# Last stage of a Mamba, attention and mixture block: where k is rotated, how q is split, and which loads go ahead of the store

## The chip, the cores and the metric

The kernel runs on one core of a Trainium2 chip. The metric is the device time of one execution in microseconds (us), as the median of several runs. Lower is better.

## The reference

The input x has 32 sequences of 64 tokens with 512 features. Three residual layers follow each other, each behind a layer norm (the third is the mixture of 64 experts of rank 8, of which 16 are chosen per token):

```python
x = x + mamba(layernorm(x), in_proj_w, conv_w, ..., out_proj_w)
x = x + cross_attention(layernorm(x), ctx, ctx, pos, mask, Wq, Wk, Wv, Wo)
x = x + experts(layernorm(x), A_w, B_w, Wq_w, keys)

def cross_attention(query, key, value, position_ids, src_mask, Wq, Wk, Wv, Wo):
    q = (query @ Wq).reshape(nb, q_len, 32, 128)
    k = (key @ Wk).reshape(nb, q_len, 8, 128)
    v = (value @ Wv).reshape(nb, q_len, 8, 128)
    q = q * cos + rotate_half(q) * sin
    k = k * cos + rotate_half(k) * sin
    scores = q @ k.T / sqrt(128); scores[mask == 0] = -1e9
    return (softmax(scores) @ v) @ Wo
```

Everything is fp32. This case is about the cross attention of the last block of tokens.

## The kernel before

**Tiling.** The 2048 tokens are four blocks of 512. `one(i, mamba, attn, nxt)` is one stage on every engine: it does the Mamba layer of block i together with attention and mixture of block i-1. `iterations` (L420) calls it five times: i = 0 (Mamba alone), i = 1 and 2 (both, a hardware loop), i = 3 (both, with no next block), and i = 4, the **last stage**, with attention and mixture of block 3 alone (`mamba` is False there). The five engine programs are written out by hand and meet only in semaphores. Each engine works strictly in its own written order. A `Stage` counts events: `x.upto(block, n)` is the count after event n of a block.

**Attention.** The 32 query heads go in 16 pairs, two pairs for each of the 8 heads of k and v. `step(jj, p, tail)` (PE: L1587, ACT: L893, DVE: L1252, SP: L548) handles pair 2jj+p. In this text a half is one such step, **even half** for p = 0 and **odd half** for p = 1. In a step PE transposes the probabilities of this pair (`turn_probs`, L1531), adds the output product of the pair before (`project_o`), makes the scores of the next pair (L1526), multiplies the probabilities with v (`values`) and makes the q of the pair after that (`project_q`, L1479). ACT copies q out of PSUM with its halves swapped (`swap_q`), takes the exponentials and copies the result of `values` out (`evac_o`). DVE, in its order, masks the scores (L1187), takes their maximum (L1193), inverts the sums of the exponentials (L1197), scales the probabilities (`probs`, L1201), makes the low part of the output (`o_low`, L1242, tile oT_lo), rotates the q of two pairs ahead (`rope_q`) and, at the end of an even half, rotates the **next k** (`rope_k`, L1172: three 128x512 operations, L1142, L1143 and L1146, the third behind a wait for the other two). The k of jj+1 is read by the scores that PE makes in the odd half. In the last stage k and v come from DRAM, where the first stage had put them.

**Two parts.** In the last stage the products are made of split operands. A matrix is written as a high part (rounded to the fp32r type) and a low part (what is left), and three matmuls stand for one fp32 matmul (`PASSES`). The activations q are split as a whole (tiles qT_hi and qT_lo, which lie over xnT and sz). The weights are split by GpSimd, whose queue is POOL: `split` (L664) makes the high part with one operation (L666, TENSOR_SCALAR) and the low part with another (L668, TENSOR_TENSOR), per step one of wq (`split_wq`) and one of wo (`split_wo`). The first wq parts lie over the first half of hs, the second over the second half, which holds the normed tokens (xn2) that PE transposes into q at the end of a stage.

**From stage 3 to the last stage.** At the end of stage 3 PE makes the mixture's A product (L1772), transposes its gated result (`zgt`), makes the B product (L1784), transposes xn2 into the PSUM tile acc (L1430, `ln2t`) and the rotary rows (L1633). ACT copies acc to qT (L804) and, in the next stage, qT to qT_hi (L922). DVE subtracts in one operation of 2048 columns (L1216). ACT then copies the rotary rows (`rop`). The first `project_q` waits for all of that and for the first split of wq.

**Loads.** SP issues the loads in its written order. `load_wa` (L443) waits until GpSimd or PE has given the buffer back. The last thing of a stage is the store of the block's result, which waits for `outr`; the first thing of the next stage is the load of the first two wq and the first wo:

```python
                if attn:
                    for n in range(2):
                        load_wa(i, n, a["wq"][n])
                    load_wb(i, 0, a["wo"][0])
...
                if attn:
                    eng.wait_ge(outr.sem, outr.upto(blk, 0))
                    eng.dma_start(out[blk], xn).then_inc(s_out, 16)
```

Of the kernel before, what the change touches and what calls it, by code (L numbers as in the profile page):

```python
# [16 lines left out]
F32 = mybir.dt.float32  # L17
# [4 lines left out]
ALU = mybir.AluOpType  # L22
ACT = mybir.ActivationFunctionType
# [7 lines left out]
TT = T // P  # L31
NB = T // SEQ
KE = E // P
DIN, NS, KC, R = 1024, 16, 4, 32
DT_TILES = DIN // P
# [44 lines left out]
def build(nc, a, out):  # L80
    ctx = ExitStack()
    with ctx:
# [9 lines left out]
        def sem(name):  # L92
            return ctx.enter_context(nc.semaphore(name))
# [10 lines left out]
        qT = sb("qT", [P, KE, T])  # L104
# [73 lines left out]
        qT2 = over("qT_hi", [P, KE, T], "xnT", 0), over("qT_lo", [P, KE, T], "sz", 0)  # L178
# [7 lines left out]
        acc = pb("acc", [P, TT, 512])  # L186
# [2 lines left out]

        q2 = qr[:, :, :].rearrange("p h t -> p (h t)").rearrange("p (b q) -> p b q", q=2 * SEQ)  # L190

        def bank(n):

            return pq[:, n, :] if n < 2 else pk[:, n - 2, :]
# [134 lines left out]
        ordy = stage("o_ready", PAIRS)  # L329
        wod = stage("wo_done", PAIRS)  # L330

        s_acth = sem("activations_hi")
        s_actl = sem("activations_lo")
        wqh = stage("wq_hi", PAIRS)
        wqs = stage("wq_split", PAIRS)
# [17 lines left out]
        zgt = stage("z_transposed", KE)  # L353
# [8 lines left out]
        yr = stage("y_gated", DT_TILES)  # L362
        opd = stage("out_proj", TT)
# [5 lines left out]
        qTr = stage("qT_ready", KE)  # L369
# [69 lines left out]
        def _(eng):  # L439
# [3 lines left out]
            def load_wa(i, at, src):  # L443

                eng.wait_ge(wad, wa_base(i) + at + (LEAD - 1))
                eng.dma_start(wa[:, at % 2, :], src).then_inc(s_wa[at % 2], 16)
# [5 lines left out]
            def load_wb(i, at, src):  # L452
                eng.wait_ge(wbd, wb_base(i) + at + (LEAD - 1))
                eng.dma_start(wb[:, at % 2, :], src).then_inc(s_wb[at % 2], 16)
# [16 lines left out]
            def one(i, mamba, attn, nxt):  # L471
                at_z, at_x, at_a = wa_places(mamba, attn, nxt)
                at_o, at_b = wb_places(mamba, attn)
                blk = i - 1
                if attn:
                    for n in range(2):
                        load_wa(i, n, a["wq"][n])
                    load_wb(i, 0, a["wo"][0])
                if mamba:

                    eng.wait_ge(sstr.sem, sstr.upto(i, 0))
# [147 lines left out]
                if attn:  # L629
                    for n in range(W_KE):  # L630
                        load_wa(i, at_a + n, a["aw"][n])
                    for n in range(W_KE):
                        load_wb(i, at_b + n, a["bw"][n])
                if attn:
                    eng.wait_ge(outr.sem, outr.upto(blk, 0))
                    eng.dma_start(out[blk], xn).then_inc(s_out, 16)
# [6 lines left out]
        def _(eng):  # L643
# [18 lines left out]
            def one(i, mamba, attn, nxt):  # L662
# [7 lines left out]
                def split_wq(jj, o):  # L670
                    p = o % 2
                    eng.wait_ge(s_wa[p], (wa_half(i) + (o // 2 + 1) + jj) * 16)

                    eng.wait_ge(qd.sem, qd.upto(i - 1, o - 2) + jj * 2)
                    hold(eng)
                    split(wa[:, p, :], [x[:, :] for x in wq2[p]], wqh, wqs, lambda s: s.upto(0, o) + jj * 2)
                    eng.wait_ge(wqs.sem, wqs.upto(0, o) + jj * 2)
                    eng.sem_inc(wad, 1)
# [86 lines left out]
                if not mamba:  # L765

                    eng.wait_ge(yad.sem, yad.upto(i - 1, NS * NCH - 1))
                    split_wq(0, 0)
                    eng.wait_ge(ln2t.sem, ln2t.upto(i - 1, KE - 1))
                    split_wq(0, 1)  # L770
                    split_wo(0, 0)
                    steps(eng, split_step)
# [20 lines left out]
        def _(eng):  # L793
# [6 lines left out]
            def evacuate(to, banks, done, ready, b):  # L800

                for k in range(KE):
                    eng.wait_ge(done.sem, done.upto(b, k))
                    S.activation(to[:, k, :], banks(k), ACT.Copy).then_inc(ready.sem, 1)  # L804
# [15 lines left out]
            def one(i, mamba, attn, nxt):  # L820
# [94 lines left out]
                    if mamba and attn and not tail and p == 1:  # L915
                        evac_v(jj + 1)

                if not mamba:
                    eng.wait_ge(yr.sem, yr.upto(blk, DT_TILES - 1))

                    eng.wait_ge(qTr.sem, qTr.upto(blk, KE - 1))
                    S.activation(qT2[0][:, :, :], qT[:, :, :], ACT.Copy).then_inc(s_acth, 1)  # L922
                if attn:
                    prefill()
                if mamba:
# [103 lines left out]
                if attn:  # L1029
                    evacuate(zgT, bank, zgt, zgr, blk)  # L1030
                if mamba:
                    evacuate(qT, lambda k: acc[:, k, :], ln2t, qTr, i)

            iterations(eng, one)

# [2 lines left out]
        def _(eng):  # L1038
# [170 lines left out]
            def one(i, mamba, attn, nxt):  # L1209
                blk = i - 1  # L1210
                rope_q, rope_k, mask_scores, max_scores, invert_sum, probs = attention_of(blk, mamba)
                if not mamba:

                    eng.wait_ge(opd.sem, opd.upto(blk, TT - 1))
                    eng.wait_ge(s_acth, 1)
                    V.tensor_tensor(qT2[1][:, :, :], qT[:, :, :], qT2[0][:, :, :].bitcast(F32),  # L1216
                                    ALU.subtract).then_inc(s_actl, 1)
                if mamba and not attn:

                    eng.wait_ge(xnr.sem, xnr.upto(0, KE - 1))  # L1220
# [31 lines left out]
                def step(jj, p, tail):  # L1252

                    soft = attn and not (tail and p == 1)
                    if mamba:
                        if p == 0:
                            eng.wait_ge(ur.sem, ur.upto(i, NCH - 1))
                        eng.wait_ge(s_bc[p], i * (8 * NS) + jj * 16 + 16)
                        scan_input(i, jj, p, 0)
                        scan_input(i, jj, p, 1)  # L1260
                        scan(i, jj, p, 0)
                        scan(i, jj, p, 1)
                        times_c(i, jj, p, 0)
                    if soft:
                        mask_scores(jj, p + 1)
                    if mamba:
                        times_c(i, jj, p, 1)
                    if soft:
                        max_scores(jj, p + 1)
                    if mamba:  # L1270
                        scan_input(i, jj, p, 2)
                        scan_input(i, jj, p, 3)
                        scan(i, jj, p, 2)
                        scan(i, jj, p, 3)
                    if mamba:
                        times_c(i, jj, p, 2)
                    if soft:
                        invert_sum(jj, p + 1)
                    if mamba:
                        times_c(i, jj, p, 3)  # L1280
                    if soft and not mamba:
                        probs(jj, p + 1)
                    if not mamba:
                        o_low(jj, p)
                    if attn and not tail:
                        rope_q(jj, p + 2)
                        if p == 0:
                            rope_k(jj + 1)

                def scan_alone(jj, p, c):  # L1290
# [122 lines left out]
        def _(eng):  # L1413
# [3 lines left out]
            eng.wait_ge(s_ident, 2)  # L1417
            eng.wait_ge(s_init, 3)
            eng.wait_ge(s_const, 16 * 9)

            def accs(k):
                return acc[:, k, :]

            def turn(x, banks, normed, done, b):

# [36 lines left out]
            def one(i, mamba, attn, nxt):  # L1462
# [177 lines left out]
                if attn:  # L1640
                    if mamba:
                        eng.wait_ge(s_ctx, blk * 16 + 16)
                        project_v(0)
                    else:
                        eng.wait_ge(s_actl, 1)
                    eng.wait_ge(rop.sem, rop.upto(blk, 0))
                    eng.wait_ge(qTr.sem, qTr.upto(blk, KE - 1))
                    project_q(0, 0)
                    free_wa(0, 0)
# [219 lines left out]
```

## Time and profile before

| | |
|---|---|
| median of 3 runs | 2400.57 us (2399.07 to 2403.79) |
| span of the profiled execution | 2396.3 us, first to last instruction and landing (the page has no other time of that execution; the median is 4.2 us more) |
| mean granted TensorE clock | 0.942 of full |
| PE busy | 2107.1 us, 88% |
| DVE busy | 1786.4 us, 75% |
| ACT busy | 1059.8 us, 44% |
| POOL busy | 588.9 us, 25% |
| last stage | from about 2024 us to the end |

The busy shares are means over stages with different limits. The last stage is a sixth of the span: PE, DVE, ACT and POOL hand work to each other there in every half, and the waits between them, read in order of time, say more than the shares.

### The profile page before, as it was taken

The numbers are of one execution on the slowest core, as the hardware profiler recorded it, in microseconds if no ns is written. First come the engines' busy times: TensorE is split into PE (matmuls) and PEld (weight loads), VectorE is DVE, ScalarE is ACT, GpSimd is POOL, SyncE is SP. The second block draws the span as 40 slices with busy tenths as digits, with TensorE's granted clock in tenths as the row PEclk, the third lists the DMA queues.
The fourth block names the chain that finished last, engine by engine and source line by source line (L and its number), as shares of the span: only waits on it lengthen the run. The fifth ranks groups of instructions, "written<-read, shape, count | busy, mean of one in ns | idle before, by whom it ended". The sixth has DMA issues, their size and how long they took to land.

```text
span 2396.3 us, 27137 instructions
## 1 busy us (share of the span) xinstructions
PE 2107.1 (88%) x8244; PEld 1194.4 (50%) x8248; DVE 1786.4 (75%) x1801; ACT 1059.8 (44%) x2613; POOL 588.9 (25%) x405
## 2 busy tenths in 40 slices
PE   6877888989999979989999979989999987799987
PEld 2332453445555534445555534445555533577763
DVE  3499994389999975289999985279999984355533
ACT  2544441465565522365665522365655521243330
POOL 0099981001111120001111110001111120566530
PEclk9888999899999989899999989889999999799888
DMA  1468893148888771238888871238888772122210
GB/s 62 166 152 198 213 213 121 54 133 187 181 177 187 166 173 53 72 123 179 176 189 179 181 172 60 72 106 172 176 196 175 171 173 82 65 90 97 88 44 18
DMA packets 110074, 328.98 MB, mean 137 GB/s; under 512 B 12945, under 2 KB 13073, under 8 KB 107569
## 3 DMA queue, kind: packets, MB, share of 16 engines
q0 software_dynamic: 35328, 127.94, 28.7%
q1 hardware_dynamic: 68912, 189.58, 26.3%
q10 hardware_dynamic: 5760, 10.49, 1.2%
q8 instruction: 45, 0.74, 0.1%
q14 instruction: 29, 0.23, 0.0%
HBM read 183.00 MB, written 14.94 MB: 83 GB/s over the span
## 4 chain that ended last, share of the span: by engine, by line
DVE 40%; PE 31%; issue 18%; DMA 5%; ACT 3%; DVEq 1%; POOL 1%; SPq 1%; POOLq 0%; ACTq 0%; PEldq 0%
DVE hs L1130 13%; PE acc L1443 5%; DVE hs L1137 5%; DVE hs L1300 5%; PE pq L1488 4%; DMA xc<-hs 3%; DVE hs L1121 3%; DVE qr L1167 2%; PE pq L1732 2%; PE pq L1496 2%; PE pq L1526 2%; PE acc L1655 2%; PE pk L1732 2%; PE acc L1565 2%; DVE sc L1187 1%
## 5 line engine op out<-in xcount | busy, mean ns | idle before, releaser
L706 POOL DMA_DIRECT2D xc<-hs x192 | 165.8, 866 | 1301.6 <-DVE hs L1137 1263.9
L1130 DVE TENSOR_TENSOR_SCAN hs<-dA,hs 128x1024 f32<-128x1024 f32 x192 | 428.9, 2276 | 0.0
L888 ACT ACTIVATE dA<-dt,aneg 128x504 f32<-128x504 f32 x384 | 253.5, 707 | 250.9 <-DVE hs L1130 250.7
L1496 PE MATMUL pq<-qT,wa 128*128 128x512 f32 x768 | 354.8, 616 | 9.2 <-DVE sc L1187 9.2
L1576 PE MATMUL acc<-wb,oT 128*128 128x512 f32 x768 | 351.7, 602 | 3.6 <-ACT oT L876 3.6
L1137 DVE TENSOR_TENSOR hs<-hs,bc 128x1024 f32<-128x1024 f32 x256 | 307.9, 1205 | 2.2
L853 ACT ACTIVATE pr<-sc,mx 128x64 f32<-128x64 f32 x512 | 170.8, 335 | 247.4 <-DVE mx L1193 247.4
L1443 PE MATMUL acc<-xnT,wa 128*128 128x512 f32 x512 | 232.2, 607 | 11.5 <-PE acc L1443 4.4
L1496 PEld LDWEIGHTS pq<-qT,wa 128*128 128x128 f32 x768 | 146.9, 197 | 183.8 <-issue 173.7
L1121 DVE TENSOR_TENSOR hs<-u,bc 128x1024 f32<-128x1024 f32 x192 | 226.3, 1219 | 8.2 <-ACT xc L976 5.9
L1526 PE MATMUL pq<-kT,qp 128*128 128x64 f32 x1024 | 190.9, 289 | 41.2 <-DVE kT L1146 16.3
L1576 PEld LDWEIGHTS acc<-wb,oT 128*128 128x128 f32 x768 | 141.1, 193 | 147.5 <-issue 143.4
L1526 PEld LDWEIGHTS pq<-kT,qp 128*128 128x128 f32 x1024 | 159.0, 205 | 78.3 <-issue 61.2
L1443 PEld LDWEIGHTS acc<-xnT,wa 128*128 128x128 f32 x512 | 96.4, 193 | 145.5 <-issue 130.5
L1528 PE MATMUL pq<-k2T,qr 128*128 128x64 f32 x768 | 154.4, 284 | 0.0
L1528 PEld LDWEIGHTS pq<-k2T,qr 128*128 128x128 f32 x768 | 122.4, 201 | 0.0
L731 POOL TENSOR_TENSOR qp<-u,bc 128x1024 f32<-128x1024 f32 x32 | 92.9, 2904 | 107.8 <-ACT xc L976 107.6
L1187 DVE COPY_PREDICATED sc<-mask,pq 128x512 f32<-128x512 int32 x64 | 46.7, 729 | 88.3 <-PE pq L1528 45.6
L731 POOL TENSOR_TENSOR qr<-u,bc 128x1024 f32<-128x1024 f32 x32 | 100.2, 3130 | 7.6 <-DVE hs L1300 7.6
L1079 DVE SCALAR_TENSOR_TENSOR xc<-acc,cw,xc 128x504 f32<-128x504 f32 (+2 forms) x96 | 69.9, 734 | 42.1 <-ACT xc L811 39.6
L1510 PEld LDWEIGHTS pk<-wv,ctxT 128*128 128x128 f32 x768 | 87.5, 192 | 27.4 <-issue 26.4
L1510 PE MATMUL pk<-wv,ctxT 128*128 128x128 f32 x768 | 92.0, 278 | 7.7 <-ACT oT L876 7.7
(200 smaller groups left out, 3312.7 us busy)
## 6 DMA issues: line engine op xcount, KB each, us to landing
xc<-hs POOLq DMA_DIRECT2D x240, 512.0 KB, 6.9
bc<-bc_rows SPq DMA_DIRECT2D x64, 512.0 KB, 7.5
wa<-in_wq SPq DMA_DIRECT2D x64, 512.0 KB, 10.2
wb<-in_wo SPq DMA_DIRECT2D x64, 512.0 KB, 5.8
wa<-in_wx SPq DMA_DIRECT2D x16, 512.0 KB, 4.2
wa<-in_wz SPq DMA_DIRECT2D x16, 512.0 KB, 4.9
wb<-in_ow SPq DMA_DIRECT2D x16, 512.0 KB, 7.2
k<-k_rows SPq DMA_DIRECT2D x32, 256.0 KB, 11.1
```

Source lines behind the costliest of these rows:

```text
L731: G.tensor_tensor(inputs[c % 2].rearrange("p (d t) -> p d t", t=T), u[:, 2 * c:2 * c + 2, :], bc[:, p, 0:1, :].to_broadcast([P, 2, T]), AL ...
L853: ins = S.activation(pr[:, b, :], sc[:, b, :], ACT.Exp, bias=mx[:, b:b + 1], accum_out=sm[:, b:b + 1])
L888: ins = S.activation(to[:, :, 1:SEQ], dt[:, s, :].rearrange("p (b t) -> p b t", t=SEQ)[:, :, 1:SEQ], ACT.Exp, scale=aneg[:, s, bass.ds(jj ...
L1121: V.tensor_tensor(hs[:, c, :].rearrange("p (d t) -> p d t", t=T), u[:, 2 * c:2 * c + 2, :], bc[:, p, 0:1, :].to_broadcast([P, 2, T]), ALU. ...
L1130: V.tensor_tensor_scan(out=hs[:, c, :], data0=dA[:, c % 2, :], data1=hs[:, c, :], initial=0.0, op0=ALU.mult, op1=ALU.add).then_inc(scd.sem, 1)
L1137: V.tensor_tensor(h3, h3, bc[:, p, 1:2, :].to_broadcast([P, 2, T]), ALU.mult).then_inc(hcd.sem, 1)
L1443: ins = M.matmul(banks(s % 4), wa4((s // 2) % 2)[:, k, (s % 2) * P:(s % 2 + 1) * P], xnT[:, k, :], start=(k == 0), stop=(k == KE - 1))
L1496: ins = M.matmul(pq[:, h, :], wa4(p)[:, k, h * P:(h + 1) * P], qT[:, k, :], start=(k == 0), stop=(k == KE - 1))
L1510: ins = M.matmul(pk[:, 1, t * D:(t + 1) * D], ctxT[:, k, t * P:(t + 1) * P], wv[:, k, :], start=(k == 0), stop=(k == KE - 1))
L1526: ins = M.matmul(pq[:, 0, seq], qp[:, b, :], kT[:, seq], start=True, stop=not mamba)
L1528: ins = M.matmul(pq[:, 0, seq], q2[:, b, :], k2T[:, seq], start=False, stop=True)
L1576: ins = M.matmul(acc[:, t, :], oT[:, h, t * P:(t + 1) * P], wb2(o % 2)[:, h, :], start=False, stop=(stop and h == 1))
```

## The change

It has three parts.

1. **k.** In the last stage `rope_k(jj + 1)` stands in an even half between `max_scores` and `invert_sum` on DVE. It stood at the end of that half, behind `rope_q`. Stages with Mamba keep their order.
2. **q.** At the end of stage 3 ACT copies acc to qT_hi directly, four times 512 columns, behind a wait for the Mamba output (since qT_hi lies over a tile that it read). The copy to qT and the copy of 2048 columns are gone. DVE subtracts in four pieces of 512 columns, straight from acc in PSUM, each behind its own piece of ACT's.
3. **Loads.** The first two wq and the first wo of the next stage are issued at the end of a stage, ahead of the wait for the result and of its store. On GpSimd the first split of wq also waits for the first transposed piece of the mixture's gated result.

```diff
@@ SP, start of a stage
-                if attn:
-                    for n in range(2):
-                        load_wa(i, n, a["wq"][n])
-                    load_wb(i, 0, a["wo"][0])
@@ SP, end of a stage
+                if mamba:
+
+                    for n in range(2):
+                        load_wa(i + 1, n, a["wq"][n])
+                    load_wb(i + 1, 0, a["wo"][0])
                 if attn:
                     eng.wait_ge(outr.sem, outr.upto(blk, 0))
                     eng.dma_start(out[blk], xn).then_inc(s_out, 16)
@@ GpSimd
                     eng.wait_ge(yad.sem, yad.upto(i - 1, NS * NCH - 1))
+                    eng.wait_ge(zgt.sem, zgt.upto(i - 2, 0))
                     split_wq(0, 0)
@@ ACT
-                if not mamba:
-                    eng.wait_ge(yr.sem, yr.upto(blk, DT_TILES - 1))
-
-                    eng.wait_ge(qTr.sem, qTr.upto(blk, KE - 1))
-                    S.activation(qT2[0][:, :, :], qT[:, :, :], ACT.Copy).then_inc(s_acth, 1)
...
                 if mamba:
-                    evacuate(qT, lambda k: acc[:, k, :], ln2t, qTr, i)
+
+                    if not nxt:
+                        eng.wait_ge(yr.sem, yr.upto(i, DT_TILES - 1))
+                    evacuate(qT if nxt else qT2[0], accs, ln2t, qTr, i)
@@ DVE
-                    eng.wait_ge(opd.sem, opd.upto(blk, TT - 1))
-                    eng.wait_ge(s_acth, 1)
-                    V.tensor_tensor(qT2[1][:, :, :], qT[:, :, :], qT2[0][:, :, :].bitcast(F32),
-                                    ALU.subtract).then_inc(s_actl, 1)
+                    for k in range(KE):
+                        eng.wait_ge(qTr.sem, qTr.upto(blk, k))
+                        V.tensor_tensor(qT2[1][:, k, :], acc[:, k, :], qT2[0][:, k, :].bitcast(F32),
+                                        ALU.subtract).then_inc(s_actl, 1)
...
                     if soft:
                         max_scores(jj, p + 1)
+                    if not mamba and not tail and p == 0:
+                        rope_k(jj + 1)
...
                         rope_q(jj, p + 2)
-                        if p == 0:
+                        if mamba and p == 0:
                             rope_k(jj + 1)
@@ PE
-                        eng.wait_ge(s_actl, 1)
+                        eng.wait_ge(s_actl, KE)
```

What this does to the order of an engine, at three places. First DVE in an even half of the last stage, from the maximum to the end of the half. Before:

```order
L1193 TENSOR_REDUCE mx<-sc 128x8 [waits scores_read]
L1197 RECIPROCAL sm<-sm 128x8 [waits exp_done]
L1201 TENSOR_TENSOR pr<-pr,sm 128x512 [waits sum_inverted]
L1247 TENSOR_TENSOR oT_lo<-pk,oT_hi 128x512 [waits o_ready]
L1247 TENSOR_TENSOR oT_lo<-pk,oT_hi 128x512
L1162 REGISTER_ALU
L1142 TENSOR_TENSOR qp<-pq,cosT 128x2x8x64 [waits scores_done,q_swapped]
L1143 TENSOR_TENSOR qr<-qr,sinT 128x1024
L1146 TENSOR_TENSOR qp<-qp,qr 128x2x8x64 [waits q_times_sin,q_times_cos]
L1173 ISA
L1174 ISA [waits k_loaded]
L1176 ISA [waits k_halves_loaded]
```

In the changed kernel the same stretch reads (all lines of the code are two further down there):

```order
L1195 TENSOR_REDUCE mx<-sc 128x8 [waits scores_read]
L1176 ISA [waits k_loaded]
L1178 ISA [waits k_halves_loaded]
L1144 TENSOR_TENSOR kT<-k,cosT 128x512 [waits scores_done]
L1145 TENSOR_TENSOR kr<-kr,sinT 128x512
L1148 TENSOR_TENSOR kT<-kT,kr 128x512 [waits k_times_sin,k_times_cos]
L1199 RECIPROCAL sm<-sm 128x8 [waits exp_done]
L1203 TENSOR_TENSOR pr<-pr,sm 128x512 [waits sum_inverted]
L1249 TENSOR_TENSOR oT_lo<-pk,oT_hi 128x512 [waits o_ready]
```

The three operations of k now stand ahead of the inversion, the scaling and the low part of the output.

Second ACT at the end of stage 3, from the copy of q. Before:

```order
L804 ACTIVATE qT<-acc 128x512 [waits ln2_transposed] x4
L922 ACTIVATE qT_hi<-qT 128x2048 [waits qT_ready,y_gated]
L846 ACTIVATE sc<-zeros 128x512 [waits exp_done]
L933 ACTIVATE cosT<-pq 128x512 [waits rotary_transposed]
L934 ACTIVATE sinT<-pq 128x512
```

In the changed kernel:

```order
L808 ACTIVATE qT_hi<-acc 128x512 [waits ln2_transposed,y_gated]
L808 ACTIVATE qT_hi<-acc 128x512 [waits ln2_transposed] x3
L850 ACTIVATE sc<-zeros 128x512 [waits exp_done]
L932 ACTIVATE cosT<-pq 128x512 [waits rotary_transposed]
L933 ACTIVATE sinT<-pq 128x512
```

The copy of 2048 columns is gone from between the copies of q and those of the rotary rows.

Third SP from the mixture's weights of stage 3 on. Before:

```order
L454 DMA wb<-in_bw 128x1024 [waits wb_used] x2
L636 DMA out<-dt 128x4x512 [waits out_ready]
L446 DMA wa<-in_wq 128x1024 [waits wa_used] x2
L454 DMA wb<-in_wo 128x1024 [waits wb_used]
L502 DMA xa<-xr 128x2048 [waits out_ready,ln2_done]
```

In the changed kernel:

```order
L456 DMA wb<-in_bw 128x1024 [waits wb_used] x2
L448 DMA wa<-in_wq 128x1024 [waits wa_used] x2
L456 DMA wb<-in_wo 128x1024 [waits wb_used]
L639 DMA out<-dt 128x4x512 [waits out_ready]
L500 DMA xa<-xr 128x2048 [waits out_ready,ln2_done]
```

The store and its wait for the result now stand behind the three loads.

## Rows read from the trace of the kernel before

**Rows 1.** Chain of waits, 1850 us to the end: shares by line.

```profile
by line: PE pq L1488 18.6%; issue 13.0%; PE acc L1565 7.0%; DVE hs L1130 6.9%; PE pq L1526 6.4%; PE acc L1772 5.2%; PE pk L1552 3.7%; PE pq L1784 2.7%; PE pq L1732 2.7%; DMA xc<-hs 2.5%; PE pk L1784 2.5%; PE pk L1732 2.5%; DVE hs L1137 2.3%
```

**Rows 2.** Timeline of PE, into the last stage: start, us, line, tiles, count, [idle before].

```profile
2006.89 1.44 PE L1430 MATMUL pq<-ident,dt 128*128 128x128 f32 x8
...
2026.30 1.04 PE L1633 MATMUL pq<-ident,oT 128*128 128x128 f32 x8
2037.47 0.77 PE L1488 MATMUL pq<-qT_hi,wq_hi 128*128 128x512 f32 x1 [10.13 <-POOL wq_lo L668]
...
2052.04 3.68 PE L1526 MATMUL pq<-kT,qp 128*128 128x64 f32 x16 [6.50 <-DVE qp L1146]
```

**Rows 3.** Timeline of ACT, same place.

```profile
2025.19 2.07 ACT L804 ACTIVATE qT<-acc 128x512 f32<-128x512 f32 x4 [15.19 <-PE acc L1430]
2027.35 1.91 ACT L922 ACTIVATE qT_hi<-qT 128x2048 fp32r<-128x2048 f32 x1
...
2030.16 0.59 ACT L934 ACTIVATE sinT<-pq 128x512 f32<-128x512 f32 x1
```

**Rows 4.** Timeline of DVE, same place.

```profile
2029.37 2.29 DVE L1216 TENSOR_TENSOR qT_lo<-qT,qT_hi 128x2048 fp32r<-128x2048 f32 x1 [4.25 <-ACT qT_hi L922]
...
2032.18 1.53 DVE L1143 TENSOR_TENSOR kr<-kr,sinT 128x512 f32<-128x512 f32 x1
```

**Rows 5.** Timeline of SP's queue, same place.

```profile
2025.59 1.56 SPq L446 DMA_DIRECT2D wa<-in_wq  x2
```

**Rows 6.** Timeline of POOL, same place.

```profile
2031.90 3.00 POOL L666 TENSOR_SCALAR wq_hi<-wa 128x1024 fp32r<-128x1024 f32 x1 [41.89 <-DMA wa<-in_wq]
2034.99 2.34 POOL L668 TENSOR_TENSOR wq_lo<-wa,wq_hi 128x1024 fp32r<-128x1024 f32 x1
```

**Rows 7.** Windows of the last stage: stretch, length, busy of PE, PEld, DVE, ACT, POOL, clock, DMA, GB/s.

```profile
2073.41:2108.90 35.49, 33.41 (x173) 27.60 (x175) 16.96 (x21) 12.73 (x42) 10.50 (x4) 0.91 0.24 82
2108.90:2312.47 203.57, 187.87 (x1009) 154.32 (x1008) 104.52 (x126) 76.41 (x252) 122.21 (x46) 0.94 0.23 79
2193.52:2208.48 14.96, 14.84 (x86) 12.34 (x87) 7.20 (x9) 6.37 (x21) 8.79 (x4) 1.00 0.57 194
2260.95:2278.77 17.82, 17.80 (x85) 15.03 (x85) 8.03 (x9) 6.37 (x21) 8.56 (x4) 0.81 0.39 133
2278.77:2296.22 17.45, 14.87 (x85) 12.11 (x85) 9.73 (x12) 6.37 (x21) 12.55 (x5) 1.00 0.25 90
```

**Rows 8.** Who waited for whom, 2108.9 to 2312.4 us: total us, times, longest.

```profile
PE pq L1526 <- DVE kT L1146: 14.4, 6, 2.4
```

**Rows 9.** Timeline of DVE, one even half (scores begin at 2278.77 us).

```profile
2281.78 0.69 DVE L1193 TENSOR_REDUCE mx<-sc 128x8 f32<-128x512 f32 x1
2285.30 0.20 DVE L1197 RECIPROCAL sm<-sm 128x8 f32<-128x8 f32 x1 [2.83 <-ACT pr L853]
...
2286.26 1.29 DVE L1247 TENSOR_TENSOR oT_lo<-pk,oT_hi 128x512 fp32r<-128x512 f32 x2
...
2294.73 1.34 DVE L1146 TENSOR_TENSOR kT<-kT,kr 128x512 f32<-128x512 f32 x1
```

**Rows 10.** Timeline of POOL, the same half.

```profile
2281.80 2.39 POOL L668 TENSOR_TENSOR wo_lo<-wb,wo_hi 128x1024 fp32r<-128x1024 f32 x1
2284.56 2.77 POOL L666 TENSOR_SCALAR wq_hi<-wa 128x1024 fp32r<-128x1024 f32 x1 [0.37 <-POOL wo_lo L668]
```

**Rows 11.** Timeline of PE, the same half: the turn of the probabilities.

```profile
2287.70 0.63 PE L1537 MATMUL pk<-ident,pr 128*128 128x128 f32 x4 [0.16 <-DVE oT_lo L1247]
```

**Rows 12.** Timelines of DVE and of POOL, an odd half in which they meet.

```profile
2232.95 2.66 DVE L1201 TENSOR_TENSOR pr<-pr,sm 128x512 f32<-128x512 f32 x1
...
2232.68 2.39 POOL L668 TENSOR_TENSOR wq_lo<-wa,wq_hi 128x1024 fp32r<-128x1024 f32 x1
```

**Rows 13.** Timeline of PE, the first wait for k.

```profile
2093.97 1.97 PE L1526 MATMUL pq<-kT,qp 128*128 128x64 f32 x16 [1.92 <-DVE kT L1146]
```

**Rows 14.** Page, part 5: the q product of the stages with Mamba.

```profile
L1496 PE MATMUL pq<-qT,wa 128*128 128x512 f32 x768 | 354.8, 616 | 9.2 <-DVE sc L1187 9.2
```

More of the change, by code:

```diff
@@ L190, in build, with accs @@
         q2 = qr[:, :, :].rearrange("p h t -> p (h t)").rearrange("p (b q) -> p b q", q=2 * SEQ)
+        def accs(n):
+            return acc[:, n, :]
         def bank(n):
@@ L330, in build @@
         wod = stage("wo_done", PAIRS)
-        s_acth = sem("activations_hi")
         s_actl = sem("activations_lo")
@@ L1419, in _ @@
             eng.wait_ge(s_const, 16 * 9)
-            def accs(k):
-                return acc[:, k, :]
             def turn(x, banks, normed, done, b):
```

## The prediction

> **What bounds the kernel now.** I read the chain of waits first, for the part that the change can touch. Its largest shares behind 1850 us are matmuls of the last stage on PE, L1488 (q) before all [rows 1]. So there PE, with what it waits for, is the bound. Then I read the timelines engine by engine at the two places of the change, and the windows for the price of a half.
>
> At the entry PE has its last work of the old stage at 2026.30 us, 1.04 us long, then nothing until 2037.47: 10.13 us of idle time, ended by GpSimd's low part of the first wq [rows 2]. GpSimd could not be earlier. It had waited for the load of wq [rows 6], which SP issued at 2025.59, behind the store of the result [rows 5].
>
> In the steady part the time goes in pairs of halves. Six pairs, from 2108.90 to 2312.47 us, take 203.57 us, 33.9 each [rows 7]. The reader is to see two things. Six times PE waits for the rotated k, 14.4 us in all [rows 8]; this ends each even half (17.45 us long, 14.87 busy at full clock, the last of rows 7). And the half behind such a wait is sometimes slow: 14.96 us at a granted clock of 1.00, but 17.82 at 0.81 [rows 7], with nothing else changed. Undisturbed, then, a half is 14.9 us at 2.4 GHz, and the wait for k is paid twice: as idle time, and as a lower clock behind it.
>
> **The change, part by part.**
>
> *The loads.* In the stages with Mamba nothing waits for the first wq: all idle time before their q product is put down to DVE's mask [rows 14]. I count nothing there; the cover is the 18 us or so of other products between load and use. Before the last stage the wq buffer is free when the A product ends, about 2000 us; the load then lands some 20 us before it is needed. The new wait on GpSimd is for the transposed z, about 2007.6 us [rows 2]; the split of 5.4 us (2031.90 to 2037.33) [rows 6] ends by about 2013, while DVE waits for the B product. Behind GpSimd's new wait stands only its own second split, which needs the transposed tokens anyway. The store is now behind the wo load, whose buffer is free halfway through the B product, about 2018 us, still before the result. So 0 for the store.
>
> *q.* With wq ready, what is late next? Before, ACT copies until 2027.26, spends 1.91 us on the copy of 2048 columns, and ends the rotary rows at 2030.75 [rows 3]; DVE's subtraction ends at 2031.66 [rows 4]. Now the 1.91 us go, and the rotary rows end at about 2028.9. DVE's four pieces follow ACT's one by one; the last starts at 2027.3. The trace has no such piece. Its price lies between 0.57 us (a quarter of the 2.29 [rows 4]) and 0.69 (512 columns with one operand in PSUM go at about half of 1.29 for two, pipelined [rows 9]), so it ends by 2028.1 either way, under ACT's rotary rows. PE starts at about 2029.0 instead of 2037.47: **8.5 us**.
> The idle time in front falls from 10.13 to about 1.7 us. Behind 10.13 us the product took 8.1 us (24 matmuls, half of them at the low clock); 24 at the pitch of the full clock take 5.7. Behind the one idle time of 1.92 us in this trace the next half stayed fast: scores of 1.97 us [rows 13]. Bounds for the gain: 0 and 2.4; I take **2.2**, since 1.7 lies nearest to 1.92. Together 10.7 us, up to the first scores, 2052.04 before [rows 2]. What GpSimd does moves along with it and starts its second split at 2026.5, not 2037.7, so it is ready everywhere.
> Rotating the first k (L1143 took 1.53 us, held up by wq_hi [rows 4, 6]) meets GpSimd again, but ends by 2034.5, before q is swapped. Cost 0.
>
> *k.* The three operations now start when the maximum ends, 3.7 us after the scores began (2282.47 less 2278.77), while DVE has 2.83 us of idle time before the inversion [rows 9]. Alone they would take about 2.05 us (three times the 0.69 of 512 columns [rows 9], some 0.1 less where the next one follows at once, and 0.1 for the wait ahead of the third), and be hidden; their loads are there a whole pair early. But they all read two tiles of SBUF, and GpSimd splits wo and wq at just that time: wo_lo from 2281.80 to 2284.19, then wq_hi from 2284.56 [rows 10]. What happens then is shown elsewhere: a DVE operation of two SBUF inputs that began in wq_lo took 2.66 us in place of 0.69, and ended 0.54 us after wq_lo did [rows 12]. Against a wq_hi that had begun it was milder: L1143 of k took 1.53 us and ended 1.81 us after wq_hi began [rows 4, 6]; at the old place the third operation of k took 1.34 [rows 9].
> So, with scores at 0: the first operation is held until wo_lo ends (5.42) and ends at 5.96. wq_hi asked at 5.79, goes next, and the second operation ends at about 7.5, the third at 8.2. Inversion and scaling, before from 6.53 on, now run from 8.2 to 9.1, and the low part of the output (1.29 us, one input in PSUM, not held up) ends near 10.45 instead of 8.78 [rows 9]. PE's turn of the probabilities already hung on that by 0.16 us, at 8.93 [rows 11]; it moves to 10.6. Everything of PE behind it moves too, so an even half takes 14.9 + 1.7 = **16.6 us**, with 1.85 us idle in another place. rope_q isn't the bound then: q is swapped at 10.97 and ready at 14.7.
> The rule for this is in the Trainium skill, SBUF — State Buffer, section Who interferes with whom: a VectorE instruction with two SBUF inputs contends with a GpSimd instruction that reads SBUF, and the one that started first keeps the shared port to its end. The 2.66 us agree; the 1.53 and 1.34 do not, for there GpSimd let go after about 1 us. By the rule taken whole the time would be 2415, a rival below.
>
> *Sum.* Entry 10.7. First pair, 35.49 us [rows 7]: GpSimd is idle at its maximum (10.50 us busy in all), so k is hidden, 1.92 goes: **2.0**. Six pairs: 6 x (16.6 + 14.9) = 189.0 against 203.57: **14.6**. All 27.3 us off the profiled span of 2396.3, so 2369.0. The median of the runs is 4.2 above that span, and stays so: **2373**.
>
> **The rivals.**
> - *No collision.* If k gets through at once, as its rows alone would have it, an even half is 14.9 too: six pairs 178.8, gain 24.8 + 2.0 + 10.7 = 37.5, time **2363**. For it: 2.05 us fit under 2.83. Against it: rows 12.
> - *The clock falls at the new place.* 1.85 us idle in each even half may lower the clock as the waits for k did, which costs up to 17.82 - 14.96 = 2.9 us. Half of that six times, 8.6: **2382**; all of it, 17.2: 2390. For it: waits of up to 2.4 us did so. Against it: the 1.92 of rows 13 did not.
> - *The entry gives little.* The first product waits for something not seen, and only the clock and a few us come: gain 18 or so, **2382**.
> - *GpSimd keeps the port (slower).* If wq_hi holds the second operation to its own end, that one ends at 9.35; wq_lo goes next, 2.35 us, the third ends at 12.3, the low part of the output at 14.6, and the turn comes at 14.75, 5.8 late. An even half is then 20.7, six pairs 213.6, 10.0 more than before, less 12.7: -2.7; and 5.8 us of idle time bring the low clock, 6 x 2.9 = 17.4 more: **2415**. It decides by 0.35 us: the scaling must ask for the port (about 8.45) before wq_lo does (8.8). If only the scaling loses that race, the turn comes at 13.15, the six pairs cost 15.3 more than I count (2389), and with the low clock 2406. For it: rows 12 show just this loss once. Against it: the shorter holds of rows 4 and 9, and the order of the requests.
> The page's rule named above is this rival in its full form.
>
> **How the numbers follow.** A measurement here can tell about 0.2% from no change, 4.8 us. Chances: forecast 0.47, no collision 0.20, low clock 0.13, weak entry 0.05, GpSimd keeps the port 0.15 (half of it in the full form). The time is the forecast's, 2373. The range from 2361 to 2392 takes in no collision, low clock and weak entry, 0.85 in all with some of it at the edges, and leaves out most of the last rival. Faster by over 0.2%: 0.86, all but the last. Within 0.2%: 0.06, its middle. Slower: 0.08, its full form.
>
> **What would show it.** The wait of 10.13 us gone, the first L1488 near 2029 us, SP's wq load near 2000. No wait of PE for kT. In even halves the first operation of k about 2.3 us long, and a wait of PE's turn for oT_lo of 1.5 to 2 us, six times: if those operations take 0.69, the first rival holds. An L1201 of over 2 us in even halves shows the slower one. A pair of 31.5 us is right, 29.8 or over 33 wrong. A gain or loss before 2000 us would be outside all of this.

## The result, and the profile after

| | before | changed |
|---|---|---|
| median of 4 runs | 2399.82 us (2398.57 to 2403.79) | 2377.28 us (2373.41 to 2379.91) |
| ratio | | 0.9902, 95% interval 0.9881 to 0.9923 |
| span of the profiled execution | 2396.3 us | 2373.8 us (own time 2375.59) |

The changed kernel is 1.0% faster. It was predicted at 2373.0 with a range from 2361 to 2392. The time comes from both places, but not in the amounts that were forecast. The two profiled spans, cut at the last rotary turn of stage 3 (the transposition of the rotary rows on PE), at the starts of the scores, and at the end:

| stretch | before | changed | gain | predicted |
|---|---|---|---|---|
| start of the program to the rotary turn | 2026.30 | 2028.20 | -1.9 | 0 |
| rotary turn to first scores | 25.74 | 14.87 | 10.9 | 10.7 |
| first scores to second | 21.37 | 19.89 | 1.5 | 0 |
| first pair | 35.49 | 34.62 | 0.9 | 2.0 |
| six pairs | 203.57 | 194.51 | 9.1 | 14.6 |
| last scores to the end | 83.8 | 81.7 | 2.1 | 0 |

**The entry.** The timeline of PE in the changed kernel, the same place as [rows 2] (start, us, line, tiles, count, idle before):

```profile
2028.20 1.04 PE L1634 MATMUL pq<-ident,oT 128*128 128x128 f32 x8
2030.81 0.47 PE L1489 MATMUL pq<-qT_hi,wq_hi 128*128 128x512 f32 x1 [1.57 <-ACT sinT L933]
2031.11 0.40 PE L1489 MATMUL pq<-qT_lo,wq_hi 128*128 128x512 f32 x1
...
2043.07 0.69 PE L1527 MATMUL pq<-kT,qp 128*128 128x64 f32 x2 [6.53 <-DVE qp L1148]
```

The idle time before the first q product is 1.57 us instead of 10.13, and what ends it is now ACT's rotary row. The matmuls that follow take 0.47 and 0.40 us; behind the long idle time they had begun at 0.77. Why, the other engines show, DVE against [rows 4], SP's queue against [rows 5], POOL against [rows 6]:

```profile
2027.78 2.48 DVE L1218 TENSOR_TENSOR qT_lo<-acc,qT_hi 128x512 fp32r<-128x512 f32 x4 [0.76 <-ACT qT_hi L808]
...
2001.53 7.56 SPq L448 DMA_DIRECT2D wa<-in_wq  x2
2019.14 0.33 SPq L456 DMA_DIRECT2D wb<-in_wo  x1
2027.05 0.40 SPq L639 DMA_DIRECT2D out<-dt  x1
...
2010.01 2.80 POOL L669 TENSOR_SCALAR wq_hi<-wa 128x1024 fp32r<-128x1024 f32 x1 [18.09 <-PE pq L1431]
2012.89 2.34 POOL L671 TENSOR_TENSOR wq_lo<-wa,wq_hi 128x1024 fp32r<-128x1024 f32 x1
```

SP issues the load 24 us earlier, GpSimd has the split ready at 2015.2, and the last of DVE's four pieces ends at 2030.26, ahead of PE. What is left is ACT's copy of the rotary rows.

**The steady part.** Windows of the changed kernel: the first pair's two halves, two even halves and one odd half behind it, and the six pairs (columns as in [rows 7]):

```profile
2062.96:2082.43 19.47, 19.47 (x89) 16.15 (x89) 9.07 (x12) 6.36 (x21) 0.00 (x0) 0.78 0.28 81
2082.43:2097.58 15.15, 14.58 (x85) 12.16 (x84) 7.69 (x9) 6.37 (x21) 10.35 (x4) 1.00 0.26 88
2097.58:2115.70 18.12, 16.19 (x85) 13.29 (x84) 11.71 (x12) 6.36 (x21) 10.57 (x4) 0.91 0.27 88
2130.87:2147.40 16.53, 14.59 (x85) 12.15 (x84) 11.72 (x12) 6.37 (x21) 10.58 (x4) 1.00 0.31 97
2147.40:2162.54 15.14, 14.57 (x85) 12.16 (x84) 7.67 (x9) 6.37 (x21) 10.34 (x4) 1.00 0.25 88
2097.58:2292.09 194.51, 179.94 (x1010) 149.27 (x1009) 115.85 (x126) 76.42 (x252) 120.38 (x46) 0.97 0.25 83
```

The odd halves are all alike now, 15.15 us at full clock; five of the six behind the first pair are so, the last, with no wq left to split, is 14.70. The even halves come in two kinds, with the same instructions in them: three of 18.1 us at a clock of 0.91, three of 16.53 at 1.00. Their mean is 17.34, as good as that of before (17.37): **the even halves gained nothing, the odd ones gained it all** (16.56 before on average, 15.08 now), since ahead of them there is no wait for k any more. Before, five of the six odd halves behind such a wait ran at a clock of 0.81 to 0.90 and took 16.2 to 17.8 us; now none does.

Who waited for whom, 2050 to 2300 us, against [rows 8]:

```profile
PE pk L1538 <- DVE oT_lo L1249: 15.0, 12, 1.9
```

PE no longer waits for kT at all. It waits at the turn of the probabilities, twelve times from the odd half of the first pair on: 1.93 us in even halves, 0.57 in odd ones. The last odd half has no such wait. The timelines of one even half (scores begin at 2097.58), DVE against [rows 9]:

```profile
2100.49 0.69 DVE L1195 TENSOR_REDUCE mx<-sc 128x8 f32<-128x512 f32 x1
2101.09 2.65 DVE L1144 TENSOR_TENSOR kT<-k,cosT 128x512 f32<-128x512 f32 x1
2103.66 1.52 DVE L1145 TENSOR_TENSOR kr<-kr,sinT 128x512 f32<-128x512 f32 x1
2105.29 0.69 DVE L1148 TENSOR_TENSOR kT<-kT,kr 128x512 f32<-128x512 f32 x1
2105.90 0.20 DVE L1199 RECIPROCAL sm<-sm 128x8 f32<-128x8 f32 x1
2106.13 0.69 DVE L1203 TENSOR_TENSOR pr<-pr,sm 128x512 f32<-128x512 f32 x1
2106.74 1.28 DVE L1249 TENSOR_TENSOR oT_lo<-pk,oT_hi 128x512 fp32r<-128x512 f32 x2
```

POOL against [rows 10], and PE against [rows 11], with three of the matmuls behind the turn:

```profile
2100.80 2.39 POOL L671 TENSOR_TENSOR wo_lo<-wb,wo_hi 128x1024 fp32r<-128x1024 f32 x1
2103.55 2.82 POOL L669 TENSOR_SCALAR wq_hi<-wa 128x1024 fp32r<-128x1024 f32 x1 [0.37 <-POOL wo_lo L671]
2106.45 2.59 POOL L671 TENSOR_TENSOR wq_lo<-wa,wq_hi 128x1024 fp32r<-128x1024 f32 x1
...
2108.17 0.63 PE L1538 MATMUL pk<-ident,pr 128*128 128x128 f32 x4 [1.93 <-DVE oT_lo L1249]
...
2109.10 0.48 PE L1566 MATMUL acc<-wo_lo,oT_hi 128*128 128x512 f32 x1
2109.38 0.63 PE L1566 MATMUL acc<-wo_hi,oT_hi 128*128 128x512 f32 x1
...
2112.98 0.39 PE L1566 MATMUL acc<-wo_hi,oT_hi 128*128 128x512 f32 x1
```

The first operation of k lasts 2.65 us: it starts 0.29 us after wo_lo and ends 0.55 us after it. The second takes 1.52 and the third 0.69, as worked out. The turn stands at +10.59. Then seven matmuls take 0.63 us and one 0.54 in place of 0.39. From 2109.38 to 2112.75 us the granted clock was 0.51, the level of 1.2 GHz, and this half took 18.12 us instead of 16.53.

### The profile page after: what moved, and what is told of

Its sections match the earlier page's. It is cut to its first block, busy times and chain, and to the rows that moved or that the text cites. A ratio compares the mean times of both kernels' runs of the same rounds, so it can differ in the third digit from the quotient of the medians.

```text
span 2373.8 us, 27142 instructions
## 1 busy us (share of the span) xinstructions
PE 2096.9 (88%) x8248; PEld 1187.8 (50%) x8248; DVE 1799.3 (76%) x1804; ACT 1057.8 (45%) x2612; POOL 587.2 (25%) x405
## 4 chain that ended last, share of the span: by engine, by line
DVE 39%; PE 30%; issue 17%; DMA 7%; ACT 4%; DVEq 1%; SPq 1%; POOL 1%; POOLq 0%; ACTq 0%; PEldq 0%
DVE hs L1132 13%; DMA xc<-hs 5%; PE acc L1444 5%; DVE hs L1139 5%; DVE hs L1304 4%; PE acc L1566 3%; DVE hs L1123 3%; PE pq L1497 2%; DVE qr L1169 2%; PE acc L1577 2%; PE acc L1656 2%; PE pq L1733 2%; PE pq L1527 2%; PE pk L1733 2%; DVE sc L1189 2%
## 5 line engine op out<-in xcount | busy, mean ns | idle before, releaser
L1538 PE MATMUL pk<-ident,pr 128*128 128x128 f32 x256 | 42.6, 291 | 82.5 <-ACT pr L865 60.7
```

## The experiments

All ratios are against the kernel before, with their 95% intervals, which reach about 4 to 9 us to either side. Times of stretches come from one profiled execution of each kernel; runs of one and the same kernel differ by 5 to 18 us.

### Which part brings what

**The changed kernel with k back at its old place.**

```diff
-                    if not mamba and not tail and p == 0:
-                        rope_k(jj + 1)
...
-                        if mamba and p == 0:
+                        if p == 0:
                             rope_k(jj + 1)
```

> The changed kernel with the rotation of the next k back at the end of the even half; the new q split and the early loads stay. Theory (the parts add up: entry 10.9 us, faster halves about 10 us): the wait of 10 us ahead of the first q product is still gone (about 1.6 us), PE waits 2.3 us for kT in seven halves again, time 2400 - 11 to 12.5 = 2387.5 to 2389. Rival (the k part carries it all, and the entry only shifts time): 2397 or more.

Measured 2384.79 us (2379.45 to 2390.53), ratio 0.9939 [0.9919, 0.996]. The entry is 14.86 us long, as in the changed kernel, so it owes nothing to k. The six pairs took 206.75 us, 3.2 more than before, the first pair 39.3, 3.8 more. The time is 2.7 us below what was expected. The span is 13.6 us shorter than before, and not all of that is the entry's 10.9: the last stage also began 6.0 us earlier, which is no part of the change as far as these runs show, and the pairs gave back 7.0.

**k alone moved**: the kernel before, with the diff above the other way round.

> The kernel before with the rotation of the next k moved between maximum and inversion and nothing else. Theory: the wait of 10 us at the entry stays, no wait for kT, PE's turn waits about 1.9 us for oT_lo in six even halves, the first operation of k takes 2.65 us there; gain 9 to 12 us, time 2388 to 2391. Rival (the collision on the port gives back all that the move gains): 2398 or more.

Measured 2385.66 us (2381.0 to 2387.38), ratio 0.9938 [0.9921, 0.9954]. That is 2.3 us below what was expected. Entry 25.91 us, first pair 33.66, six pairs 196.06; the two pair stretches together are 9.3 us shorter than before. Here four of six even halves took 18.12 us and two 16.54, each with a wait of 1.93 or 1.94 in it: which ones get the low clock is not tied to the place.

**The loads alone**: SP's loads ahead of the store and GpSimd's wait for the transposed z; q and k as before.

> The kernel before with only the early loads of wq and wo (and GpSimd's wait that goes with them); q is split as before, k is rotated as before. Theory: the first q product now waits for DVE's subtraction of 2048 columns, which ended at 2031.7 us; it starts 5.7 us earlier, the clock still falls in the idle time; time 2393.5 to 2395. If GpSimd's second split, now 11 us earlier, takes the port from that subtraction (both of its inputs are in SBUF), it starts 3.4 us earlier only: 2396.5. Rival (the loads carry the whole entry, the q split nothing): 2389.

Measured 2398.67 us (2390.77 to 2402.45), ratio 0.9989 [0.9972, 1.0006]: no gain is shown, where 2393.5 to 2395, or 2396.5 with a collision, was expected, but the interval reaches to 6.7 us faster. The entry, in the timelines of PE, DVE and POOL:

```profile
2026.60 1.04 PE L1635 MATMUL pq<-ident,oT 128*128 128x128 f32 x8
2032.01 0.80 PE L1490 MATMUL pq<-qT_hi,wq_hi 128*128 128x512 f32 x1 [4.38 <-DVE qT_lo L1218]
...
2029.66 2.29 DVE L1218 TENSOR_TENSOR qT_lo<-qT,qT_hi 128x2048 fp32r<-128x2048 f32 x1 [4.25 <-ACT qT_hi L924]
...
2029.84 4.35 POOL L669 TENSOR_TENSOR wq_lo<-wa,wq_hi 128x1024 fp32r<-128x1024 f32 x1
```

The long wait becomes one of 4.38 us for the low part of q, and the entry is 20.41 us, 5.3 less. The expectation's fear came the other way round: DVE's subtraction took its 2.29 us, and GpSimd's wq_lo was held up beside it. In this execution the pairs take as much more as the entry takes less: 3.9 us in the first pair, 1.7 in the six. The windows of that pair's halves show where, with another odd half of the same kernel for comparison:

```profile
2088.86:2106.70 17.84, 17.84 (x84) 14.79 (x84) 8.84 (x9) 6.36 (x21) 8.55 (x4) 0.81 0.48 163
...
2193.03:2207.82 14.79, 14.68 (x85) 12.15 (x85) 7.21 (x9) 6.37 (x21) 8.80 (x4) 1.00 0.60 196
```

It is the half behind the first wait for k. That wait lasted 1.92 us, just as in [rows 13], and there the clock had stayed up; the 2.9 us between 17.84 and 14.96 [rows 7] are most of the pair's 3.9. This is not shown to come from the early loads: the same half took 17.82 us with k back at its old place and 17.80 with q alone (below), both at 0.81 behind 1.92 us, and q alone has no early start. Of four kernels with k at its old place, the kernel before is the only one in which it ran fast.

**The fourth run was not what its label says.** It was meant as q alone. The kernel that ran was the changed kernel with only the early loads taken back, so it held the new place of k as well. What was expected of it is therefore no test; it is read as "q and k, no loads".

```diff
+                if attn:
+                    for n in range(2):
+                        load_wa(i, n, a["wq"][n])
+                    load_wb(i, 0, a["wo"][0])
...
-                if mamba:
-                    for n in range(2):
-                        load_wa(i + 1, n, a["wq"][n])
-                    load_wb(i + 1, 0, a["wo"][0])
...
-                    eng.wait_ge(zgt.sem, zgt.upto(i - 2, 0))
```

> The kernel before with only the new q split; loads and k as before. Theory: GpSimd's first split of wq, which waits for its load, ends the wait before the first q product as before, so nothing is gained: 2399 to 2401. Rival (each part gives its own share of the entry): 2395 to 2397.

Measured 2382.0 us (2377.12 to 2384.59), ratio 0.9926 [0.9908, 0.9944]. The first q product waits 9.95 us for the split of wq, and the entry is 25.98 us. Its interval overlaps with that of k alone.

**q alone, this time indeed**: the edit above and that of the first experiment together.

> The kernel before with only the new q split; loads and k as before. (The kernel of e4_q_only also held the new place of k, so this is the run that its text meant.) Theory: GpSimd's first split of wq, which waits for its load, ends the wait before the first q product as before; the product begins 11.0 to 11.2 us after the turn of the rotary rows, as in the kernel before, and no wait changes in the halves; what is left is what the clock does, 2 us or so either way: 2396 to 2401. Rival (the split has a share of its own at the entry): the product begins 2 us earlier or more, 2395 or less.

Measured 2400.76 us (2394.25 to 2410.01), ratio 1.0016 [0.9994, 1.0038]: nothing, as expected. PE's timeline shows q's split hidden behind the load. Below it stands the window of the half behind the first wait for k:

```profile
2031.99 0.77 PE L1485 MATMUL pq<-qT_hi,wq_hi 128*128 128x512 f32 x1 [10.18 <-POOL wq_lo L670]
...
2088.94:2106.74 17.80, 17.79 (x85) 14.60 (x85) 9.32 (x9) 6.36 (x21) 8.55 (x4) 0.81 0.50 163
```

So by the medians k alone gives some 13.5 us, loads and q together 14.4, q alone nothing, and the loads alone nothing that can be told from noise. At the entry the parts are clearer: 5.3 us with the loads alone, 0.4 with q alone, 10.9 with both, since each shortens a wait that another covers. That 13.5 and 14.4 add up to more than the changed kernel's 22.5 is within the intervals, and no run tells whether the parts take from each other.

### Is it GpSimd that holds k up, and does the held time bring the low clock?

**wo_lo filled without reading.** In every even half GpSimd fills wo_lo with zeros instead of computing it, so that nothing reads SBUF there while k begins.

```diff
-                    G.tensor_tensor(two[1], raw, two[0].bitcast(F32), ALU.subtract).then_inc(both.sem, 1)
+                    if low:
+                        G.tensor_tensor(two[1], raw, two[0].bitcast(F32), ALU.subtract).then_inc(both.sem, 1)
+                    else:
+                        hold(eng)
+                        G.memset(two[1].bitcast(F32), 0.0).then_inc(both.sem, 1)
```

> The changed kernel in which GpSimd only writes zeros for the low part of wo of every second pair of heads (the split that runs in an even half while DVE rotates k), in place of the subtraction that reads SBUF; that part of wo is left out of the result. Theory (the port is what holds DVE up): the first operation of k takes 0.7 us, not 2.65; PE's turn in an even half waits 0.6 us at most, not 1.93; an even half takes 14.9 to 15.2 us in place of 16.5 to 18.1, and the time is 2377 - 10 to 15 = 2362 to 2367. Rival (k is held up by something else, such as its loads or a semaphore): rows and time as in the changed kernel, 2375 to 2379.

Measured 2358.32 us (2352.5 to 2364.13), ratio 0.9833 [0.9797, 0.9868]. DVE, POOL and the window of one even half:

```profile
2094.10 0.68 DVE L1149 TENSOR_TENSOR kT<-k,cosT 128x512 f32<-128x512 f32 x1
2094.70 0.69 DVE L1150 TENSOR_TENSOR kr<-kr,sinT 128x512 f32<-128x512 f32 x1
2095.50 1.33 DVE L1153 TENSOR_TENSOR kT<-kT,kr 128x512 f32<-128x512 f32 x1
2097.02 0.20 DVE L1204 RECIPROCAL sm<-sm 128x8 f32<-128x8 f32 x1 [0.19 <-ACT pr L862]
...
2093.87 0.96 POOL L675 MEMSET wo_lo<- 128x1024 f32 x1 [0.15 <-POOL wo_hi L669]
2095.19 2.83 POOL L669 TENSOR_SCALAR wq_hi<-wa 128x1024 fp32r<-128x1024 f32 x1 [0.36 <-POOL wo_lo L675]
...
2090.59:2105.36 14.77, 14.61 (x85) 12.12 (x84) 9.73 (x12) 6.37 (x21) 8.94 (x4) 1.00 0.37 108
```

The first operation takes 0.68 us although the MEMSET still runs when it begins. k is done before the exponentials, the inversion waits for ACT again, and an even half is 14.77 us, with a wait of 0.16 at the turn. No half behind the first pair falls below full clock: the six pairs take 179.07 us, 15.4 less than in the changed kernel, of which the waits saved in even halves are 6 x 1.77 = 10.6, and three halves without the low clock, 1.6 us each, are the rest. Both steps hold: the read of SBUF by GpSimd holds k up, and the idle time behind that brings the low clock. The time is 3.7 us below what was expected; the last stage began at 2020.7 us in this execution, 7.5 earlier than in the changed kernel, so the steps are read from the halves and not from the whole.

### A version that does the same work without the collision

**k in two pieces.** Its two products go ahead of the mask, where GpSimd is idle or has only begun wo_hi, and the difference stays behind the maximum.

```diff
+                    if not mamba and not tail and p == 0:
+                        begin_k(jj + 1)      # k1 *= cosT, kr *= sinT
...
                     if not mamba and not tail and p == 0:
-                        rope_k(jj + 1)
+                        end_k(jj + 1)        # kT = k1 - kr
```

> The changed kernel with the rotation of k in two places: its two products in place, ahead of the mask of the even half (DVE waits there for the scores, and GpSimd is at the high part, which keeps the port only about 1 us), and the difference alone between maximum and inversion. Theory: the products are done before the scores are; the difference is held until the low part of wo ends, about 6.1 us after the scores began, still ahead of the inversion at 6.5; the turn waits about 0.5 us, an even half takes 15.0 to 15.3 us, time 2362 to 2367. Rival (the turn hangs on the probabilities and the low part in another way, so that the place of k doesn't matter): 2374 to 2379.

Measured 2362.39 us (2358.72 to 2366.39), ratio 0.9842 [0.981, 0.9874], as expected. DVE in one even half (scores begin at 2097.47), and the windows of this half and of the six pairs:

```profile
2096.77 0.69 DVE L1185 TENSOR_TENSOR k<-k,cosT 128x512 f32<-128x512 f32 x1
2097.37 0.69 DVE L1186 TENSOR_TENSOR kr<-kr,sinT 128x512 f32<-128x512 f32 x1
...
2100.98 2.74 DVE L1192 TENSOR_TENSOR kT<-k,kr 128x512 f32<-128x512 f32 x1
...
2097.47:2112.46 14.99, 14.61 (x85) 12.15 (x84) 10.69 (x11) 6.37 (x21) 10.46 (x4) 1.00 0.34 106
2097.47:2277.74 180.27, 175.14 (x1009) 145.78 (x1008) 112.72 (x125) 76.44 (x252) 119.68 (x46) 1.00 0.27 89
```

One operation still meets wo_lo and is held for 2.74 us. But the other two are out of the way, so the wait at the turn is 0.36 instead of 1.93, and every half behind the first pair runs at full clock.

**The same, with wq split only after q is ready.**

```diff
+                    eng.wait_ge(qrdy.sem, qrdy.upto(0, o - 2) + jj * 2)
+                    hold(eng)
```

> The kernel of e6_k_in_two, in which GpSimd's split of wq also waits until DVE has rotated the q that was made of the buffer's last content. Theory: in the first step GpSimd's low part of wq no longer takes the port from the rotation of q (3.2 us for the second product there, 1.2 alone), so PE's wait of 7.4 us falls to 5.4 and the scores of the second pair begin 2 to 2.7 us earlier; in the steady halves the wait is over when the split's turn comes, and nothing moves. Time 2362.4 - 2 to 3 = 2359.5. Rival (the later splits are then late for the q product, and PE waits for wq_lo): 2363 or more, with a wait of the q product for GpSimd.

Measured 2357.39 us (2352.98 to 2362.9), ratio 0.9842 [0.9821, 0.9862]. From first scores to second it takes 18.39 us instead of 21.08. 2.0 us of that are L1147 (sin times q), which takes 1.21 us; in the changed kernel it took 3.22 beside GpSimd's split. The rest is mostly the clock. The halves behind it are no shorter (six pairs 180.90): the wait at the turn in odd halves grew from 0.57 to 0.72, where no change was expected. With the same ratio as the version before, this second step is not shown to gain; k in two pieces is, and both beat the changed kernel (their intervals end below its 0.9881).

## Why the prediction was right, and where it was not

- **Entry, 8.5 + 2.2: right.** From rotary turn to first q product it was 11.17 us and is 2.61, a gain of 8.56; the rest, 2.3, is the clock behind it. The loads-only run, in which PE waited 4.38 us for the low part of q, shows that both edits were needed.
- **No cost at the store or at the new wait: right.** GpSimd's split ended 15 us before PE used it. The new wait itself was taken away in no run.
- **First operation of k held to 5.42 and ended at 5.96, the third ending at 8.2, the turn at 10.6 behind 1.85 us: right.** wo_lo ended 5.61 us behind the scores and the first operation at 6.16, the third at 8.40; the turn came at 10.59 behind 1.93 us. The 0.35 us by which the scaling comes before wq_lo were 0.32. The slower rival, which lives on that margin, did not come about in any of the six pairs, and "no collision" was refuted by the 2.65 us.
- **"An even half takes 16.6 us": the step that failed.** Three of six did (16.53); the others took 18.1. The forecast had taken one wait of 1.92 us with a fast half behind it [rows 13] as a sign that 1.85 us are safe. That was the exception: the same wait was followed by 17.8 us at 0.81 in all three other kernels that have it (loads alone, k back, q alone). So the second rival, the clock falling at the new place, which had been given 0.13, was half true: half as often, and at 1.6 us each, not 2.9, since the low clock lasted for some eight matmuls (8 x 0.2 us). That is 4.8 us.
- **"Odd halves 14.9": 15.15.** Before, L1201 took 0.69 us in most halves. Now wq_hi starts 0.3 us before it in each, it takes 1.28 us, and PE waits 0.57. Five times 0.25, 1.3 us.
- **First pair 2.0: 0.9.** Its wait for k is gone, but its even half ran at a clock of 0.78 where it had been 0.84 before, and its odd half took 0.2 us more. That even half took 18.5 to 19.7 us over all kernels with the new place of k, so its price is no constant.
- **"All before 2000 us unchanged" and the tail.** The last stage began 1.9 us later, and over all kernels here between 2020.3 and 2028.2 us, early loads or not (2028.2, 2020.3, 2026.6, 2020.7, 2027.9 and 2022.8 with them, 2026.3, 2024.5, 2023.4 and 2020.8 without). This is larger than several of the terms; its cause stays open, and each figure is of one execution. The tail was 81.6 to 84.7 us with the same work. In the stretch from 38 to 58 us behind the last scores the clock was 0.97 in the changed kernel and 0.93 before; that is all that is shown of it. The stretch from the first scores to the second, 1.5 us shorter, comes from two things. The second q product waited 0.95 to 0.97 us for the mask in all seven kernels with the new split of q, and 1.31 to 1.33 in the three without: 0.35 us that no part of the sum had; why the mask comes sooner is not shown. The other 1.1 us are the clock. Of that product's 24 matmuls, 13 took 0.6 us or more before and 7 in the changed kernel; over all kernels it was 6 to 14, with no part of the change that decides it.

The sum was 27.3 us, and 22.5 came by the spans: 6.7 too much in the pairs, 1.9 for the later start, against 3.6 not foreseen between the first scores and the second and in the tail, and 0.2 more at the entry. The errors cancelled in part: that the time was met more closely than the terms is luck.

## What to carry to other kernels

When a wait is covered by another that ends a few microseconds earlier, the two edits must be judged together: alone each may measure as nothing, and that tells nothing against it. Before moving a DVE operation with two SBUF inputs into a gap, lay GpSimd's timeline beside it; a gap of 2.83 us was too small for 2.05 us of work, and moving two of three operations by a few microseconds brought the gain that moving them all had missed. And a short wait of PE has a second price in the clock that comes in some instances only: price it with a chance, and look at all such waits in the trace, not at the one that was safe.

## What the runs showed of the hardware

- Two GpSimd operations on tiles of the same size hold DVE for different times. Begun inside a TENSOR_TENSOR, a DVE operation of two SBUF inputs ended 0.55 us after it (2.65 and 2.74 us instead of 0.69). Beside a TENSOR_SCALAR that lasted 2.8 us it took 1.52, 1.33 or 1.28 us, and ended 1.19 us before it each time. A third operation of k, begun 1.74 us into such a TENSOR_SCALAR (2105.29 against 2103.55), took its 0.69 us. So the TENSOR_SCALAR holds DVE up in its first part only. The Trainium skill, SBUF — State Buffer, section Who interferes with whom, says that a GpSimd instruction that only writes SBUF does not contend; the 0.68 us beside the MEMSET agree.
- It goes both ways: where DVE's subtraction began 0.18 us before, GpSimd's wq_lo took 4.35 us instead of 2.34.
- Waits of PE at the turn of 0.16 to 0.73 us, ten to twelve in each of the last three kernels (wo_lo not read, k in two pieces, wq after q), never came with a granted clock below 1.00 in their half. Waits of 1.91 to 1.94 us there came with one of 0.91 in 10 of 18 (changed kernel, k alone, and q and k without loads), between the same instructions. Waits for k of 2.3 to 2.5 us came with 0.75 to 0.90 in the half behind them in 19 of 24 (the kernel before, k back, loads alone, q alone).
